# Two-layer decoder: compact key and query projections spread by small DMAs, loads issued inside the first attention stage

## What is computed

```
q = norm(x_b) Wq + bq        [112, 16]     k = ctx_b Wk + bk  [375, 16]     v = ctx_b Wv  [375, 16]
p = exp(q k^T / 4 - rowmax)  [112, 375]    o = (p v) / rowsum(p)            x_b += concat_h(o) Wo + bo
```

## Time and profile before

| | us |
|---|---|
| median of 3 runs | 1895.57 (1894.42 to 1898.14) |
| the profiled execution's own time | 1894.81 |
| its span | 1892.7 |
| TensorE busy | 1486.7 (79%) |
| VectorE busy | 803.2 (42%) |
| ScalarE busy | 585.1 (31%) |
| GpSimd busy | 400.4 (21%) |

### The profile page before, as it was taken

One profiled execution on the slowest core, in us unless ns is written; L12 is line 12 of the kernel. 1 busy time (PEld: TensorE's weight loads), 2 busy tenths in 40 slices (PEclk: granted clock), 3 DMA queues, 4 the chain that ended last, 5 costly groups with the idle time before them and its releaser, 6 DMA issues. The chain is left out here.

```text
span 1892.7 us, 36157 instructions
## 1 busy us (share of the span) xinstructions
PE 1486.7 (79%) x14148; PEld 1154.7 (61%) x14148; DVE 803.2 (42%) x1935; ACT 585.1 (31%) x1278; POOL 400.4 (21%) x488
## 2 busy tenths in 40 slices
PE   0688778999997749999945666659999998659993
PEld 0355546666666539999923554536676676549991
DVE  1355535555552152222255666644545543132226
ACT  0166614454453112222201111214555554112220
POOL 0366510000000124444353111100000000124424
PEclk9999969999997569999956888859999998559995
DMA  7000000000000139999820000000000000139972
GB/s 186 18 1 2 2 1 2 1 2 2 2 2 1 39 144 321 333 322 328 297 66 18 0 0 0 1 1 1 2 2 2 2 2 2 39 143 325 330 251 81
DMA packets 47134, 154.82 MB, mean 82 GB/s; under 512 B 6208, under 2 KB 28064, under 8 KB 32673
## 3 DMA queue, kind: packets, MB, share of 16 engines
q0 software_dynamic: 21120, 130.53, 19.3%
q1 hardware_dynamic: 19868, 19.42, 3.4%
q10 hardware_dynamic: 6020, 3.07, 0.6%
HBM read 140.16 MB, written 12.85 MB: 81 GB/s over the span
## 5 line engine op out<-in xcount | busy, mean ns | idle before, releaser
L849 DVE TENSOR_REDUCE xa_mx<-xa_ps_s 112x2 f32<-112x750 f32 x256 | 240.4, 939 | 259.3 <-PE xa_ps_s L611 259.0
L617 PE MATMUL xa_ps_p<-xa_qs,xa_kT 32*125 32x112 f32 x3072 | 241.7, 289 | 59.8 <-DVE xa_mx L849 48.7
L617 PEld LDWEIGHTS xa_ps_p<-xa_qs,xa_kT 32*125 32x125 f32 x3072 | 198.5, 190 | 140.8 <-issue 69.5
L769 ACT ACTIVATE xa_p<-xa_ps_p 125x672 f32<-125x672 f32 x256 | 186.9, 730 | 226.2 <-PE xa_ps_p L617 226.2
L611 PE MATMUL xa_ps_s<-xa_kT,xa_qT 32*112 32x375 f32 x1024 | 232.6, 530 | 9.4 <-DVE xa_mx L849 9.2
L1443 PEld LDWEIGHTS ex_ps_h<-ex_xT,ex_w 128*128 128x128 f32 x1792 | 214.4, 196 | 10.1 <-DMA ex_w<-in_experts1a,ex_now 3.7
L1443 PE MATMUL ex_ps_h<-ex_xT,ex_w 128*128 128x128 f32 x1792 | 215.0, 279 | 6.5 <-DMA ex_w<-in_experts1a,ex_now 3.3
L1454 PE MATMUL ex_ps_y<-ex_w,ex_hT 128*128 128x256 f32 x896 | 202.7, 379 | 0.0
L1454 PEld LDWEIGHTS ex_ps_y<-ex_w,ex_hT 128*128 128x128 f32 x896 | 165.9, 190 | 20.2
L1477 ACT ACTIVATE ex_hT<-ex_ps_h,ex_w 128x128 f32<-128x128 f32 x224 | 70.0, 364 | 288.0 <-PE ex_ps_h L1443 288.0
L1489 DVE TENSOR_SCALAR ex_hT<-ex_ps_h,ex_w 128x128 f32<-128x128 f32 x224 | 68.2, 346 | 165.2 <-PE ex_ps_h L1443 165.2
(11 more groups left out here) (261 smaller groups left out, 2224.9 us busy)
## 6 DMA issues: line engine op xcount, KB each, us to landing
ys<-ex_y SPq DMA_DIRECT2D x56, 128.0 KB, 4.5
xn<-rt_xn SPq DMA_DIRECT2D x8, 448.0 KB, 4.4
load_cin<-in_ctx ACTq DMA_DIRECT2D x4, 750.0 KB
x<-in_x SPq DMA_DIRECT2D x1, 1792.0 KB, 16.2
out_x<-x SPq DMA_DIRECT2D x16, 112.0 KB, 1.9
wq_x<-in_wq_x SPq DMA_DIRECT2D x2, 512.0 KB
w_l<-in_w_l SPq DMA_DIRECT2D x1, 1024.0 KB
ex_xg<-xn,ex_now POOLq DMA_INDIRECT x56, 4.8
```

The lines of the kernel that those rows point to most:

```text
L617: return pe.matmul(bp[0:CT, i, c * S:(c + 1) * S], kT[r:r + 32, b % KB, n, c * CT:(c + 1) * CT], qs[r:r + 32, b % 2, n, :], start=True, st ...
L769: act.activation(p[slot % 4][:, :, :], bp[0:CT, :, 0:NC3 * S], ACT.Exp).then_inc(exped, 1)
L849: dve.tensor_reduce(mx[:, b % 2, 2 * pair:2 * pair + 2], bsc[0:S, :, 0:CL], AX, ALU.max).then_inc(maxed, 1)
```

## The change

Keys and queries are projected without padding, to 256 rows: two key matmuls and four query matmuls an element. They are copied to compact tiles `kU` and `qU` (the queries' factor 1/4 is now applied in that copy, by VectorE in both layers), and SyncE moves each head's 16 rows to its strip of 32 with DMAs: 16 for the keys of an element, 8 for the queries, one that clears the query rows for the shift, and 4 that later put the shift there. The key tile's other rows are set to one once, by GpSimd. The second query tile is gone: minus the maximum is turned by one transpose of [112, 16], copied by ScalarE to `nmT` and moved by DMA into row 16 of the query strips. Rounds wait for the DMAs' semaphores. The pieces between the rounds stand in another order, and x is turned one step earlier, so the loop begins at -3.

The stage `load_constants` is gone. SyncE issues the loads in the line attention stage: x in four parts, then the four loads that line attention needs, then those of cross attention, the context among them (already turned by the host), then the rest. The statistics of x are taken in four groups, their scales by GpSimd in four groups; each constant row is made in the stage that uses it.

```diff
--- before.py
+++ after.py
...
-    g.wq_x = sb("wq_x", [P, 2, 2, PW])
-    g.wk_x = sb("wk_x", [P, 2, PW])
+    g.wq_x = sb("wq_x", [P, 2, 2, D])
+    g.wk_x = sb("wk_x", [P, 2, D])
...
+def load_constants(sp, g, A):
+
+    for n in range(4):
+        rows = slice(4 * n, 4 * n + 4)
+        sp.dma_start(g.x[:, rows, :], A["x"][rows].rearrange("b t d -> t b d")).then_inc(g.x_in[n], 16)
+    sp.dma_start(g.w_l0[:, :, :], A["w_l0"].rearrange("(c p) n -> p c n", p=P)).then_inc(g.line_in, 16)
+    sp.dma_start(g.wo_l0[:, :, :], A["wo_l0"].rearrange("(c p) n -> p c n", p=P)).then_inc(g.line_in, 16)
+    sp.dma_start(g.bv[:, :], A["bv"]).then_inc(g.line_in, 16)
+    sp.dma_start(g.rows[:, :, :], A["rows"].rearrange("(o r) d -> o r d", o=1)).then_inc(g.line_in, 16)
...
+    sp.dma_start(g.bk_x[:, :, :], A["bk_x"]).then_inc(g.cross_in, 16)
+    for n in range(4):
+        sp.dma_start(g.cT[:, 4 * n:4 * n + 4, :], A["ctxT"][:, 4 * n:4 * n + 4, :]).then_inc(g.cross_in, 16)
...
+    sp.wait_ge(g.cross_in, 16 * CROSS_DMAS)
+    sp.wait_ge(g.rest_in, 16 * REST_DMAS)
...
+                if b == 0:
+                    pe.wait_ge(g.line_in, 16 * LINE_DMAS)
...
+            def constant_row():
+                pe.wait_ge(spread, 1)
+                for c in range(2):
+                    pe.matmul(b_out[0:S, 0:D], g.bvb[:, c, :], g.wo_l0[:, c, :], start=(c == 0), stop=False)
+                pe.matmul(b_out[0:S, 0:D], g.ones[0:1, 0:S], g.rows[0:1, 0, :], start=False, stop=True).then_inc(crow_made, 1)
...
+                if t == 0:
+                    constant_row()
+                    pe.wait_ge(set_v, 5)
+                    pe.wait_ge(set_p, 2)
...
+            def row_stats(n):
+                dve.wait_ge(g.x_in[n], 16)
+                for b in range(4 * n, 4 * n + 4):
+                    dve.bn_stats(first_stats[:, b, :], g.x[:, b, :]).then_inc(x_read, 1)
+                for b in range(4 * n, 4 * n + 4):
+                    dve.wait_ge(x_read, b + 1)
+                    dve.bn_aggr(g.mv[:, b, :], first_stats[:, b, :]).then_inc(x_known, 1)
...
+                if t < 3:
+                    row_stats(t + 1)
+                if t == 1:
+                    dve.wait_ge(crow_made, 1)
+                    dve.tensor_copy(g.crow[:, 0, :], b_out[0:S, 0:D]).then_inc(crow_set, 1)
...
+    kU = ph.sb("kU", [P, 2, 2, CL])
+    qU = ph.sb("qU", [P, 2, 2, S])
+    bqs = ph.sb("bqs", [P, 2])
+    kT = ph.sb("kT", [P, RB, QUADS, CL])
+    qT = ph.sb("qT", [P, RB, QUADS, S])
+    zeros = ph.sb("zeros", [4, QUADS, S])
...
+        @block.sync
+        def _(sp):
+            def spread_k(b, m):
+                sp.wait_ge(k_copied, 2 * b + m + 1)
+                reused(sp, shifted, PAIRS * (b - RB + 1))
+                sp.wait_ge(ones_set, b % RB + 1)
+                for k in range(2):
+                    for j in range(4):
+                        i = 4 * k + j
+                        sp.dma_start(kT[32 * j:32 * j + HD, b % RB, 2 * m + k, :], kU[HD * i:HD * i + HD, b % 2, m, :]) \
+                            .then_inc(k_spread[RB * m + b % RB], 16)
+
+            def spread_q(b):
+                sp.wait_ge(q_copied, b + 1)
+                reused(sp, shifted, PAIRS * (b - RB + 1))
+                sp.wait_ge(zeros_set, 2)
+                sp.dma_start(qT[HD:P:32, b % RB, :, :], zeros[:, :, :]).then_inc(q_spread[b % RB], 16)
+                for k in range(2):
+                    for j in range(4):
+                        i = 4 * k + j
+                        sp.dma_start(qT[32 * j:32 * j + HD, b % RB, k:QUADS:2, :], qU[HD * i:HD * i + HD, b % 2, :, :]) \
+                            .then_inc(q_spread[b % RB], 16)
+
+            def spread_nm(b):
+                sp.wait_ge(nm_copied, b + 1)
+                reused(sp, shifted, PAIRS * (b - RB + 1))
+                for j in range(4):
+                    sp.dma_start(qT[32 * j + HD:32 * j + HD + 1, b % RB, :, :], nmT[QUADS * j:QUADS * j + QUADS, b % 2, :]) \
+                        .then_inc(nm_spread[b % RB], 16)
+
+            for t in range(-2, NB):
+                if on(t + 2):
+                    spread_k(t + 2, 0)
+                    spread_q(t + 2)
+                if on(t + 1):
+                    spread_nm(t + 1)
+                if on(t + 2):
+                    spread_k(t + 2, 1)
...
             def round_of(t, slot):
-                sb, sp = (t + 1, slot + 3) if slot < 5 else (t + 2, slot - 5)
+                sb, sp = ahead(t, slot)
                 if on(t):
                     if slot == 0:
-                        pe.wait_ge(qs_made, t + 1)
+                        pe.wait_ge(nm_spread[t % RB], 16 * NM_DMAS * (t // RB + 1))
                     reused(pe, exped, PAIRS * t + slot)
                 if on(sb):
                     if sp == 0:
-                        pe.wait_ge(q_copied, sb + 1)
-                    if sp % 2 == 0:
-                        pe.wait_ge(k_copied, QUADS * sb + sp // 2 + 1)
+                        pe.wait_ge(q_spread[sb % RB], 16 * Q_DMAS * (sb // RB + 1))
+                    if sp % 4 == 0:
+                        pe.wait_ge(k_spread[RB * (sp // 4) + sb % RB], 16 * K_DMAS * (sb // RB + 1))
                     reused(pe, maxed, PAIRS * sb + sp)
...
+            def keys(b, m):
+                if m == 0:
+                    reused(pe, k_copied, 2 * b)
+                else:
+                    reused(pe, v_copied, NC3 * b)
+                    pe.wait_ge(k_copied, 2 * b + 1)
+                pe.matmul(bk[:, 0:CL], g.wk_x[:, layer, m * P:(m + 1) * P], g.cT[:, b, :],
+                          start=True, stop=True).then_inc(k_made, 1)
...
             def shift_turn(b):
                 pe.wait_ge(nm_set, b + 1)
-                pe.wait_ge(v_copied, NC3 * b + 2)
-                for n in range(QUADS):
-                    last = pe.transpose(ba[1][:, n * S:(n + 1) * S],
-                                        nmp[:, 4 * n:4 * n + 4, :].rearrange("t h e -> t (h e)"), g.ident[0:S, 0:S])
-                last.then_inc(nm_turned, 1)
+                pe.wait_ge(v_copied, NC3 * (b + 1))
+                pe.transpose(bx[0:H, 0:S], nm[:, :], g.ident[0:S, 0:S]).then_inc(nm_turned, 1)
...
+            for t in range(-3, NB + 1):
                 round_of(t, 0)
                 if on(t - 1):
                     values(t - 1, 3)
                 if on(t + 2):
-                    x_turn(t + 2)
+                    keys(t + 2, 0)
                 round_of(t, 1)
                 if on(t + 2):
-                    keys(t + 2, 0)
                     queries(t + 2)
                 round_of(t, 2)
                 if on(t):
                     values(t, 0)
                 if on(t - 1):
                     u_turn(t - 1)
-                if on(t + 2):
-                    keys(t + 2, 1)
                 round_of(t, 3)
-                if on(t + 2):
-                    keys(t + 2, 2)
+                if on(t + 1):
+                    context_values(t + 1, 0)
+                    context_values(t + 1, 1)
                 round_of(t, 4)
                 if on(t):
                     values(t, 1)
-                if on(t - 1):
-                    out_turn(t - 1)
+                if on(t + 1):
+                    context_values(t + 1, 2)
+                round_of(t, 5)
                 if on(t + 2):
-                    keys(t + 2, 3)
-                round_of(t, 5)
+                    keys(t + 2, 1)
                 if on(t + 1):
-                    context_values(t + 1, 0)
-                    context_values(t + 1, 1)
+                    shift_turn(t + 1)
                 round_of(t, 6)
                 if on(t):
                     values(t, 2)
                 if on(t - 1):
+                    out_turn(t - 1)
+                round_of(t, 7)
+                if on(t + 3):
+                    x_turn(t + 3)
+                if on(t - 1):
                     out_product(t - 1)
...
+            def shift_copy(b):
+                act.wait_ge(nm_turned, b + 1)
+                if b >= 2:
+                    act.wait_ge(nm_spread[(b - 2) % RB], 16 * NM_DMAS * ((b - 2) // RB + 1))
+                act.activation(nmT[:, b % 2, :], bx[0:H, 0:S], ACT.Copy).then_inc(nm_copied, 1)
...
+                if layer == 0:
+                    dve.scalar_tensor_tensor(qU[:, b % 2], made, CROSS_SCALE, bqs[:, :].unsqueeze(2).to_broadcast([P, 2, S]),
+                                             ALU.mult, ALU.add).then_inc(q_copied, 1)
+                else:
+                    dve.tensor_scalar(qU[:, b % 2], made, CROSS_SCALE, None, ALU.mult).then_inc(q_copied, 1)
...
+                    if slot == 0 and on(t - 2):
+                        finish(t - 2)
+                    if slot == 1 and on(t + 2):
                         q_copy(t + 2)
                     if slot == 2 and on(t - 1):
                         normalise(t - 1)
-                    if slot == 3 and on(t + 3):
-                        normed_row(t + 3)
```

(32 more changed lines are left out.)

340 lines of the change are left out of this document (134 added, 206 removed).

## The result

| kernel | median us | lowest to highest | runs | ratio to before, 95% interval |
|---|---|---|---|---|
| before | 1895.65 | 1894.42 to 1898.14 | 4 | |
| after | 1985.87 | 1980.83 to 1992.41 | 4 | 1.0479 [1.0453, 1.0504] |

The kernel is 4.8% slower, 90 us; forecast were 1752 us and a range up to 1808. The span of the profiled execution is 1983.8 us.

What follows compares the result with a forecast made beforehand. TensorE was taken to bound cross attention. From 1894.8 us, 88 came off for shorter periods and 56 for earlier loads, nothing for the ramps: 1750.8, as a median 1752, range 1728 to 1808.

Steps and rivals of the forecast that it cites:

- What bounds the kernel: Cross attention: TensorE bounds it, 20.26 us a period of eight slots; each slot costs 2.03 or its TensorE work.
- part 1: Cross-attention period: fewer projections, query products and shift transposes save 2.77 us of TensorE work; reordered slots sum to 16.50.
- The floor of 16.5: Cross-attention period in us if DMAs are never late; with loads gaining 60, time 1730, chance 0.12.
- Part 2: Cross-attention DMA waits: period 17.1 us (ends 16.5 and 19.35) instead of 20.26, a gain of 88 us.
- p = 0.37: SyncE's assumed pitch in us between small DMA issues, from 0.32 in the result's stores plus a small gap.
- My own two lines: Period sum: queries land 3.15 + 16p + 1.9 after slot 0, shift 3.05 + 3p + 1.9 after slot 5; 17.1 us.
- rival (b): Cross attention: DMA pace sets the period, pitch 0.45 and landing 2.3 give 19.35 us; time 1814, chance 0.17.
- Rival (c): Cross attention: pitch 0.60 gives period 22.2, and the low clock adds 1.5 a period; time 1935, chance 0.06.
- Rival (a): Cross attention: waits at slot 5 or 0 drop TensorE's clock, two rounds a period at half speed; 1785, chance 0.15.
- Part 3: Ramp of each cross-attention layer: no change taken, bounds 2 us gained to 5 lost a layer.
- Part 4: Loads at the start: first projection moves from 75.74 to about 15 us; net gain 56, ends 46 and 60.
- my own break-even: Where the slower case starts to lose: a period of 22.3 us without the clock, or p near 0.55 with it.

Runs made afterwards that it cites:

- e7: After with all 16 key, four of eight query and two of four shift DMAs issued by GpSimd, constant query DMA ahead of the projection wait; 1806.07 us.
- e6: After with all 16 key and two of eight query DMAs issued by GpSimd, constant query DMA ahead of the projection wait; 1788.14 us.
- e4: After with idle TensorE matmuls, 17 before slot 1 and 4 before slot 5, to keep the clock up; 1989.43 us.
- e1: Loads and line attention of after with the cross attention of before, no DMA between copy and score; 1839.43 us.
- m1: Separate program without the decoder that times groups of eight small DMAs by kind and issuing engine; 110.33 us.
- e9: e7 with 64 idle 1 x 1 matmuls ahead of each layer's loop, meant to move the instruction fetches; 1806.34 us.

## Why the prediction was wrong

**What bounds the kernel** and **part 1** held. Slots 5 to 0 of after come 2.03 to 2.09 apart, as the pieces said, and where the DMAs are in time e7's later periods reach 17.3 and e6's shortest 16.85. The floor of 16.5 itself is not seen.

**Part 2 failed, by its pitch.** I took p = 0.37 from the stores of the result, whose DMAs have device memory on one side. The kind of DMA that the change adds costs 0.57 to 0.59 to issue, 0.62 to 0.64 with its gap, and 0.72 in the period shown with the long issues among them (0.70 over all periods, by 24.1 = 4.4 + 28p). The bounds, 0.32 to 0.45, left it out. The row of 0.56 in the same group is a load from device memory behind other loads; it is near the right number without being of the right kind. The Trainium skill's 512 cycles (DMA: Bandwidth & Descriptors, Why a DMA increments its semaphore by 16 and not by 1), an estimate of 0.43 us with the clock of Advanced Engine Details and Errata (Clock Domains), are nearer than my value and still too low by 0.14 to 0.3 in these runs.

The pitch alone turns the sign. My own two lines with the measured 0.72 and 1.9 give 3.15 + 11.52 + 1.9 = 16.57 and 3.05 + 2.16 + 1.9 = 7.11: a period of 23.7 where before has 20.26, a loss of 96 us in 28 periods. The traces show 105.

The shape of the sum was wrong as well, but small. I timed the queries from the start of slot 0, with 17 DMAs ahead of their landing, as if SyncE were free when the first key half is copied. It is free only if the second key half of the batch before has gone out. The whole loop, slot 5 to slot 5, has 29 DMAs: 2.5 + 28p + 1.9. At my p it is 14.8 and hides under 17.1; above p = 0.45 it is over that, and above 0.62 it is over my own lines as well (10.0 + 19p). At 0.72 it is 24.6, 0.9 more than they give. The landing, 1.9, was right, so rival (b) fell on p alone.

**Rival (c)** had the mechanism and the sign, and 1935 for the time, at a chance of 0.06. Its second term, 1.5 us a period for the low clock after a long wait, appeared in the trace (2.97 + 2.61 against 2 x 2.03) and cost nothing that can be measured, since the loop hardly passes through those rounds (e4). So its 1935 has 42 us for the clock that did not come, and is too low all the same: by the pitch, 0.72 for 0.60, and by the ramps. Rival (a) fell too. It asked whether half a microsecond of waiting drops the clock: waits of 1.46 and 1.59 at slot 5 left the next rounds 2.04 and 2.03 apart, and the 0.86 comes from the long wait at slot 1, as a symptom. The Trainium skill (TensorE: Matmul & The Clock Gate, HAM oscillation) warns of DMA waits in a loop that take the clock down each turn; the rounds at 402.16 and 404.77 agree, and e4 shows that removing it was worth nothing here.

**Part 3 failed with it**: I took 0, bounds -2 to 5; against e1 it is 15.9 in the first layer and 14.8 in the second. The ramp fills three batches through the same queue. Its row of 16 key DMAs takes 13.29 us in after:

```profile
216.75 13.29 SPq L618 DMA_DIRECT2D xa_kT<-xa_kU  x16
```

**Part 4 was right**, in part by luck: 56.2 measured (e1), 56 forecast. The first projection came at 12.64 against 15, a gain of 63.1 for 60.7, and the 3.2 us that the ramp of the first cross attention lost in e1 were in no term. The sum had +56 and +88; it got +56, -105 for the periods, -31 for the ramps and about -11 for the rest.

The sign hung on a price that no row showed. I had bounded it by rows of another kind of DMA, and gave 0.94 to a gain that by my own break-even needed a p under about 0.55 (its lines give 0.52 with the low clock and 0.60 without).

## What to carry to other kernels

Where many small DMAs join a loop, find or measure the price of one issue of the same kind (which memory on each side, which issuing engine) before anything else; a price of another kind turned the sign here. Then write the loop of the *issuing* queue: all its DMAs of a period times the pitch, plus one wake-up and one landing, from a consumer to the same consumer a turn later. That is a floor for the period beside that of each engine, and a queue in order lets a batch's early transfers stand behind the last one's late transfers. Spread such DMAs over idle engines before judging the idea: here the same arithmetic went from 4.8% slower to 5.7% faster by issuing 18 of 29 elsewhere.

## What was not expected of the hardware

- Issue time goes by the kind: on-chip to on-chip 0.57 to 0.61 us on SyncE and ScalarE (0.50 for 4 rows of 448 bytes), 0.48 to 0.52 on GpSimd; with device memory on one side 0.32 alone, 0.42 to 0.45 in a row. From 16 to 128 rows it hardly changes (m1: 5.03 and 5.08 us for eight on the chip, 3.57 and 3.81 to device memory).
- Two engines issue side by side at nearly full pace: 5.29 and 5.00 us for eight each, 5.03 and 5.02 alone (m1).
- A clock bought back in rounds off the loop (0.85 to 0.95 in the stretch, e4) gave no time.
- DMA issues and landings that are 0.5 to 2 us late come together with an instruction fetch: all 38 SyncE issues of over 0.75 us in after (up to 2.06), and all 28 waits of 1 to 2 us at slot 1 of e7 and e9. That the fetch is the cause is not shown, and before one wait of e6 the pause begins ahead of the fetch.
